# Attention in a decoder layer: softmax row sums taken two chunks later in one pass, with the joined pairs added by DMA, and TensorE's value products cut in quarters

## What is computed

```python
x = _layernorm(x + _L0_attn_ref(x, L0_attn_w_qkv, L0_attn_w_out, L0_attn_b_out), axis=-1)
x = _layernorm(x + _L0_xattn_ref(x, ctx_1024, ctx_1024, L0_xattn_W_out), axis=-1)
x = _layernorm(x + _L0_ffn_ref(x, L0_ffn_clip_x, L0_ffn_clip_down, L0_ffn_w_gate, L0_ffn_w_up, L0_ffn_w_down), axis=-1)
```

```python
dots = jnp.einsum('bhnd,bhmd->bhnm', q, k) * SCALE
attn = jax.nn.softmax(dots, axis=-1)
out = jnp.einsum('bhnm,bhmd->bhnd', attn, v)
```

## Time and profile before

| what | us |
|---|---|
| median of 3 runs (1819.03 to 1823.56) | 1822.68 |
| the profiled execution, its own time | 1825.24 |
| its span in the trace | 1823.4 |
| TensorE busy | 1770.6 |
| VectorE busy | 1450.9 |
| ScalarE busy | 1445.7 |
| GpSimd busy | 194.8 |

### The profile page before, as it was taken

The page is one execution under the profiler, slowest core; times in us unless marked ns, Lnnn a source line. Parts: engine busy times, 40 slices in busy tenths (PEclk is TensorE's granted clock), DMA queues, the critical chain, the costliest instruction groups (busy, mean ns, idle before and its releaser), DMA issues. The chain is left out here.

```text
span 1823.4 us, 40231 instructions
## 1 busy us (share of the span) xinstructions
PE 1770.6 (97%) x15938; PEld 900.4 (49%) x15938; DVE 1450.9 (80%) x1582; ACT 1445.7 (79%) x1581; POOL 194.8 (11%) x189
## 2 busy tenths in 40 slices
PE   8999999999999999999999999999989999999997
PEld 6887885333333333333333333333346776644443
DVE  5345345988998898899998999989984778788898
ACT  5344356999999999999999999999964555555487
POOL 0000000010010010010010010010112221000044
PEclk9999999999999999999999999999999999999999
DMA  8665556658567577477566667676556340122075
GB/s 295 212 236 205 199 204 198 139 123 191 128 142 180 120 160 174 114 164 177 128 150 169 146 148 177 136 179 149 117 143 212 139 138 24 64 127 127 1 293 209
DMA packets 110832, 288.79 MB, mean 158 GB/s; under 512 B 8676, under 2 KB 25188, under 8 KB 97252
## 3 DMA queue, kind: packets, MB, share of 16 engines
q1 hardware_dynamic: 97012, 187.08, 28.7%
q0 software_dynamic: 13680, 99.62, 28.4%
HBM read 105.01 MB, written 82.05 MB: 103 GB/s over the span
## 5 line engine op out<-in xcount | busy, mean ns | idle before, releaser
L918 DVE TENSOR_TENSOR dve_sum<-dve_sum,probs 128x2048 f32<-128x2048 f32 x320 | 733.6, 2292 | 34.3 <-ACT probs L842 25.6
L842 ACT ACTIVATE probs<-score_others,shift_now 128x1536 f32<-128x1536 f32 x384 | 597.4, 1556 | 0.0
L1035 PE MATMUL mixed_ps<-probs,value_piece 128*32 128x512 f32 (+1 forms) x3840 | 402.9, 516 | 1.1 <-ACT probs L842 0.2
L841 ACT ACTIVATE probs<-score_first,shift_now 128x512 f32<-128x512 f32 x384 | 267.0, 695 | 2.2 <-PE score_others L997 1.1
L997 PE MATMUL score_first<-first_queries,key_piece 32*128 32x512 f32 x768 | 248.3, 429 | 4.3 <-ACT probs_paired L841 1.9
L997 PE MATMUL score_others<-first_queries,key_piece 32*128 32x512 f32 x2304 | 251.0, 429 | 0.0
L997 PE MATMUL score_others<-q_second,key_piece 32*128 32x512 f32 x2304 | 247.4, 424 | 0.0
L997 PE MATMUL score_first<-q_second,key_piece 32*128 32x512 f32 x768 | 245.1, 424 | 0.1
L997 PEld LDWEIGHTS score_first<-first_queries,key_piece 32*128 32x128 f32 x768 | 123.2, 185 | 186.0 <-ACT probs L841 94.9
L997 PEld LDWEIGHTS score_first<-q_second,key_piece 32*128 32x128 f32 x768 | 121.8, 183 | 183.4 <-ACT probs L841 105.4
L842 ACT ACTIVATE probs_paired<-score_others,shift_now 128x1536 f32<-128x1536 f32 x128 | 202.4, 1581 | 0.0
(11 more groups left out here) (253 smaller groups left out, 2581.7 us busy)
## 6 DMA issues: line engine op xcount, KB each, us to landing
probs_paired<-probs_paired POOLq DMA_DIRECT2D x95, 1024.0 KB, 8.4
o_scratch<-out_parts SPq DMA_DIRECT2D x33, 512.0 KB, 2.8
k_scratch<-parts SPq DMA_DIRECT2D x32, 512.0 KB, 4.6
q_scratch<-parts SPq DMA_DIRECT2D x32, 512.0 KB, 2.7
key_piece<-k_scratch SPq DMA_DIRECT2D x32, 512.0 KB, 5.1
h_scratch<-h SPq DMA_DIRECT2D x5, 2816.0 KB, 8.1
h<-h_scratch SPq DMA_DIRECT2D x5, 2816.0 KB, 11.5
v_scratch<-values SPq DMA_DIRECT2D x32, 256.0 KB, 2.0
```

Source lines behind the costliest of these rows:

```text
L841: nc.scalar.activation(block_probs(k)[:, 0:CH], score_first[:], ACT.Exp, bias=shift[:, c:c + 1], scale=SCALE).then_inc(probs_done, 1)
L842: nc.scalar.activation(block_probs(k)[:, CH:HPG * CH], score_others[n % 2][:], ACT.Exp, bias=shift[:, c:c + 1], scale=SCALE).then_inc(prob ...
L918: nc.vector.tensor_tensor(total[:], first[:], block_probs(k)[:], ALU.add).then_inc(dve_added, 1)
L1035: last = nc.tensor.matmul(mixed_ps[j * HD:(j + 1) * HD, lo:hi], v_group[k // KPP][:, k % KPP, j * HD:(j + 1) * HD], block_probs(k)[:, j * ...
```

## The change

Four things change in `attend`.

1. The pairs are blocks (8, 9) and (13, 14). The two joined pairs are no longer joined with each other; each is added by DMA onto VectorE's finished sum (`join_sum`), so a chunk has four accumulating DMAs where it had three. ScalarE waits for `pair_free`, which GpSimd raises when such a DMA has landed.
2. The sums of chunk `f - 2` (`BEHIND = 2`) are taken in one pass with ones at step 0 of chunk `f`. The values' result waits in one of two `mixed` tiles. In chunk 1, TensorE fills `mixed_ps` with ones in place of a sum. The last two chunks get their sums at the end, the very last from five passes.
3. Values start at step 1 and are issued by quarters of a block: `VALUE_PARTS`.
4. VectorE gathers after all 11 adds, not before the last. SyncE no longer waits for `four_landed`, and loads values and keys in turn.

```diff
-    PAIRS = ((2, 3), (4, 5))
+    PAIRS = ((8, 9), (13, 14))
-    SUM_PARTS = 2
-    SUMS_AT = ((0,), (1,))
+    BEHIND = 2
+    CHUNKS = ITERS * CPB
-    VALUE_HALVES = (0, 0, 2, 2, 3, 2, 2, 3, 2, 2, 3, 2, 2, 3, 2, 2)
-    HALF = CH // 2
+    VALUE_PARTS = (0, 4, 4, 5, 4, 4, 4, 5, 4, 4, 4, 5, 4, 4, 4, 5)
+    PARTS = 4
+    PART = CH // PARTS
...
-                            sp.wait_ge(four_landed, 1 + (it + 1) * CPB)
...
+                            for piece in range(PIECES):
+                                values_read(piece)
+                                load_v(ng, nb, piece)
+                                if piece + 2 < PIECES:
+                                    keys_read(piece + 2)
+                                    load_k(ng, nb, piece + 2)
...
-                            if i is not None and k == PAIRS[i][1]:
-                                act.wait_ge(pairs_landed, it * CPB + c + 1)
-                            elif i == 0:
-                                act.wait_ge(four_landed, it * CPB + c + 1)
-                            elif i == 1:
-                                act.wait_ge(sums_done, it * CPB + c + 2)
+                            if i is not None:
+                                act.wait_ge(pair_free, 2 * (it * CPB + c) + 1 + i)
...
+                def chunk(it, c, adds):
+                    take_shift(it if c == 0 else it + 1, (c + CPB - 1) % CPB)
+                    invert(it * CPB + c)
+                    divide(it * CPB + c, c)
+                    for a in range(adds):
+                        add(it, c, a)
...
+                        chunk(it, c, ADDS)
+                        gather(it, c + 1)
...
+                def join_sum(it, c, i):
+                    f = it * CPB + c
+                    pool.wait_ge(pair_joined[i], 16 * (f + 1))
+                    if i == 0:
+                        pool.wait_ge(dve_added, (f + 2) * ADDS)
+                    pool.sem_inc(may_join, 1)
+                    nc.gpsimd.dma_start(dve_sum[c % 2][:], probs_paired[i][0][:], accum_op=ALU.add).then_inc(sum_joined, 16)
+                    pool.wait_ge(sum_joined, 32 * f + 16 * (i + 1))
+                    pool.sem_inc(pair_free, 1)
...
+                def sums(f):
+                    pe.wait_ge(mixed_copied, f + BEHIND)
...
+                    elif f < BEHIND:
+                        fill().then_inc(sums_done, 1)
                     else:
...
+                        pe.wait_ge(sum_joined, 32 * (f - 1))
+                        ones_times(mixed_ps, dve_sum[f % 2], True, True).then_inc(sums_done, 1)
+                def sums_last():
+                    pe.wait_ge(mixed_copied, CHUNKS + BEHIND)
+                    pe.wait_ge(probs_done, EXPS + CHUNKS * KB * 2)
+                    raw = [*PAIRS[1], ADD_ORDER[-1]]
+                    pe.wait_ge(pair_joined[0], 16 * CHUNKS)
+                    ones_times(mixed_ps, probs_paired[0][0], True, False)
+                    for k in raw:
+                        ones_times(mixed_ps, block_probs(k), False, False)
+                    pe.wait_ge(dve_added, (CHUNKS + 1) * ADDS - 1)
+                    ones_times(mixed_ps, dve_sum[(CHUNKS - 1) % 2], False, True).then_inc(sums_done, 1)
```

More of the change, by code:

```diff
@@ L699, in attend @@
         dve_added, may_join = sem("dve_added"), sem("may_join")
-        pair_joined, four_joined = sem("pair_joined"), sem("four_joined")
-        pairs_landed, four_landed = sem("pairs_landed"), sem("four_landed")
+        pair_joined, sum_joined = [sem(f"pair_joined{i}") for i in range(len(PAIRS))], sem("sum_joined")
+        pair_free = sem("pair_free")
         mixed_copied = sem("mixed_copied")
@@ L815, in _ @@
                     sp.wait_ge(v_in[piece], 16 * ITERS)
-                store(ITERS, 0)
+                for c in range(BEHIND):
+                    store(ITERS, c)
             @block.scalar
@@ new lines, in chunk @@
+                def chunk(it, c, adds):
[4 more added lines that the diff above has]
+                        add(it, c, a)
+                with v.Fori(0, ITERS - 1) as it:
+                    for c in range(CPB):
+                        chunk(it, c, ADDS)
+                        gather(it, c + 1)
+                for c in range(CPB - 1):
+                    chunk(ITERS - 1, c, ADDS)
+                    gather(ITERS - 1, c + 1)
@@ L1025, in values, with ones_times, fill @@
-                def values(f, k, halves):
+                def ones_times(out, part, start, stop):
+                    for j in range(HPG):
+                        last = nc.tensor.matmul(out[j * HD:(j + 1) * HD, :], keep.ones[:, 0:HD], part[:, j * CH:(j + 1) * CH],
+                                                start=start, stop=stop)
+                    return last
+                def fill():
+                    for t in range(KT):
+                        last = nc.tensor.matmul(mixed_ps[:, t * P:(t + 1) * P], keep.ones[:], keep.ones[:], start=True, stop=True)
+                    return last
@@ L1042, in _ @@
                 pe.sem_inc(sums_done, 1)
-                for t in range(KT):
-                    last = nc.tensor.matmul(mixed_ps[:, t * P:(t + 1) * P], keep.ones[:], keep.ones[:], start=True, stop=True)
-                last.then_inc(filled, 1)
+                fill().then_inc(filled, 1)
                 for n in range(1, AHEAD):
@@ L1051, in _ @@
                     done = 0
-                    for step, halves in enumerate(VALUE_HALVES):
+                    for step, parts in enumerate(VALUE_PARTS):
                         if f * KB + step + AHEAD < CHUNKS * KB:
                             score(f * KB + step + AHEAD)
-                        for at in SUMS_AT[step] if step < len(SUMS_AT) else ():
-                            sums(f, at)
+                        if step == 0:
+                            sums(f)
+                        if f == CHUNKS - 1 and step == KB - AHEAD:
+                            sums_last_but_one()
                         for k in range(KB):
-                            now = [half for half in range(2) if done <= 2 * k + half < done + halves]
+                            now = [part for part in range(PARTS) if done <= PARTS * k + part < done + parts]
                             if now:
                                 values(f, k, now)
-                        done += halves
+                        done += parts
                 def first_product(t):
@@ L1066, in first_product @@
                                          start=m == 0, stop=m == len(terms) - 1)
-                for at in range(len(PAIRS) + 1):
-                    sums(CHUNKS, at, len(PAIRS) + 1)
+                sums_last()
                 pe.wait_ge(w_lo_done, ITERS)
```

142 lines of the change are left out of this document (57 added, 85 removed).

## The result

| | before | after |
|---|---|---|
| median of 5 runs each, us | 1820.06 | 1840.22 |
| lowest to highest, us | 1819.03 to 1823.56 | 1834.23 to 1843.26 |
| span of the profiled execution, us | 1823.4 | 1839.7 |
| mean granted clock of TensorE | 0.989 | 0.982 |

The ratio is 1.0098, 95% interval 1.0077 to 1.0119: the change costs 20 us. The forecast was 1807 us and faster; the median lies above the whole range.

A forecast was written before the change was run, and what follows sets the result against it. TensorE bounded the kernel by a few tenths, ScalarE right behind. 32 x 31.9 + 1.7 + 14 = 1036.5 against 1053.7, less 1.3 at the end, saves 15.9: 1807 us from the median 1822.68, range 1790 to 1833 (forecast's own 1798 to 1817).

The forecast's parts named there:

- VectorE's loop, 31.7 us, fits under.: VectorE's chunk loop: 31.7 us, under ScalarE's 31.84 by 0.15; as a rival 32.3 us, 1820 us in all, chance 0.10.
- Weight loads, 0.3 us a chunk.: TensorE's pieces of 128 columns: weight loads add 0.01 to 0.02 us a round, 0.3 us a chunk.
- That rival: Weight loads show in TensorE's quarters: 1.8 us a chunk, TensorE at 32.9, 1832 us in all, chance 0.06.
- I take 31.9, a gain of 0.68 a chunk.: Usual chunk at ScalarE's pace, 1.99 us a block or 31.84, taken as 31.9; gain 21.8 us in 32 chunks.
- Landing at 49.8, 2.0 late, 14 us in all.: Joins at an iteration's end, with one and a half loads, land 2.0 us late for block 8, at seven ends.
- the upper bound: Iteration ends cost 6 us each if about 1.5 MB of loads is paid in full, with a loss of clock.
- The second rival: turns the sign at 4.3 us each.: GpSimd's chain bounds the iteration ends: ScalarE waits at block 8, 6 us seven times, 42 for 14, 1835 us, chance 0.17.
- 1.4 us of margin: Usual chunk's joins land at 46.4 us after the chunk's start; ScalarE needs block 8's tile at 47.8.
- The start's 1.7 us stay.: Start of the attention stage: the 1.7 us beyond the chunks' pace and late sums are kept.
- 1.3 us more at the end.: End: five passes of 0.96 us for three and one more inversion; passes end at 7.8 instead of 6.5.
- the first rival: No wait at the iteration's ends: the sum without the 14 us, 1793 us, chance 0.22.

The follow-up runs named there:

- e11: Kernel of e1 with the third score product left out for one block in four; 1805.1 us, ratio to before 0.9924.
- e5: Kernel of e1 with TensorE's values in two steps of six quarters instead of four of five, the others four; 1804.6 us, ratio to before 0.9911.
- e1: Changed kernel with GpSimd's split of the weight share moved behind the issue of the first sum join of the iteration's third chunk; 1800.1 us, ratio to before 0.9894.
- e12: Kernel of e8 with its steps of nine and eight eighths strictly in turn; 1801.9 us, ratio to before 0.9900.
- e9: Changed kernel with the split, still in the open, in an iteration's first chunk instead of its third (`W_AT = 0`); 1805.4 us, ratio to before 0.9928.
- e8: Kernel of e1 with values in eighths of a block, eight nines and seven eights over steps 1 to 15; 1800.5 us, ratio to before 0.9888.
- e4: Changed kernel with the first pair at blocks 10 and 11 instead of 8 and 9; 1825.1 us, ratio to before 1.0023.

## Why the prediction was wrong

- *"VectorE's loop, 31.7 us, fits under."* Right. It waits 1.13 us for the sums in each chunk and in most 0.39 to 0.55 for the values, and ScalarE waits for it in no trace.
- *"Weight loads, 0.3 us a chunk."* Nothing: a step of 16 small matmuls takes the 1.07 us of one with 8, and e11 shows that TensorE's total does not count. That rival fell.
- *"I take 31.9, a gain of 0.68 a chunk."* Mis-sized: 0.40, 12.8 us in place of 21.8. I read 1.99 us a block from a stretch where ScalarE had work waiting. In step with TensorE a block of the new kernel takes 2.01 on average, in every table but e5's. The mechanism fits: in the rows the four steps of three halves account for before's other 0.4, and two such steps cost 0.13 in e5.
- *"Landing at 49.8, 2.0 late, 14 us in all."* **This step failed.** The place, the wait and the order of events were right; the size of this wait was not, and that took the sign with it. In the chunk shown the second join of chunk 2 landed at 24.8 (I said 23.5), the first join went out at 28.7 (27.3), and three joins with the loads took 23.9 us (19.4 and 3.1 for loads); block 8 started at 52.7 where ScalarE stood ready at 48.5 (1110.25 - 4.19, from 1057.5). I had treated the loads as a sum to add to a row of joins. The runs show a chain instead: the split starts only when the last join onto the sum has landed, and the next join onto the sum only when the first pair's has, so what a load takes from one landing is paid again in the start of the next join. The mean wait was 3.3 us, and 1.5 of after-effect followed, mostly by the lower clock, which I had priced only in the upper bound: 4.9 us seven times, 34 in place of 14.
- *"The second rival: turns the sign at 4.3 us each."* This is what happened, at 4.9. I gave it 0.17, and my range ended at 1833, under this rival's own 1835, though my own sum had 1.4 us of margin against a split and four loads. The evidence against it, that loads beside joins suffer rather than the joins, came from two joins with a gap behind them; here there are four, and the only gap is the split.
- *"The start's 1.7 us stay."* The first chunk varies between executions of nearly the same code, 31.99 (e1), 33.19 (after), 34.71 (e12), 34.84 (before); it says nothing of the change.
- *"1.3 us more at the end."* 5.3, as the split delays the last join too and the passes behind that wait run at the lower clock. In e1 it is 7.9 against 6.6: 1.3.

The traces put the miss at some 20 us at the boundaries, 8 in the usual chunks (0.26 in each of 32) and 4 at the end. With the split hidden the kernel stands at 1800 us, near the first rival's 1793 plus these 8: the idea was worth 20 us and was lost at seven places and at the end.

## What to carry to other kernels

When work is moved to a queue whose waits leave no gap, look for everything else that its engine does, however small: here 4 us of unrelated work once in 128 us decided between 20 us lost and 20 us won, and the cure was to put it behind an issue where the engine waits anyway. Price contention on a chain by following each start to the landing it waits for, rather than by adding the bytes at the end; and a margin of 1 us on transfers of 8 to 14 us is none. A pace read from a stretch in which one engine catches up is not the pace of two engines in step.

## What was not expected

- The split's subtraction takes 2466 to 2658 ns in after, where it starts within one of VectorE's adds, and 731 to 737 ns in e1, where VectorE is in a short transpose; the cast takes 0.43 to 1.81 us against 0.72. In all fourteen traces together it starts within an add 50 times, takes 2.46 to 2.71 us and ends 0.58 to 0.60 us after that add; the other 62 times it takes 0.72 to 0.74 us, once 1.00. So it waits for the add's end, and half of the 3.65 us that the split took in the chunk shown was such waiting. e1 thus moved the split to a better place in two ways, which were not told apart; e9 left it among the adds.
- In e8 and e12 block 15 takes 2.10 us in most chunks, whether the last two steps are both long or not, and the chunk still takes 32.15. Where the 0.02 us a block over 1.99 are lost was not found: after a wait whole chunks run at 1.99 to 2.01 (31.98 us in e4), and the next is back at 32.15.
- e12 waited 2.0 us at one boundary of seven although its split is hidden. What is left of the margin is small, and times of 1800 to 1802 us, or usual chunks of 32.14 to 32.16, are not to be told apart.
